# Attention block, one core: value products in two column halves of TensorE, in batches of one to five units, and VectorE normalising straight from PSUM

## The reference

```python
y = x * rsqrt(mean(x * x, -1) + eps) * rms_w           # x: 2 x 1024 x 512
y = einsum('bsm,cm->bsc', y, w_in)                      # 32 query heads, 8 groups of keys and values, 64 wide
q, k = rope(q), rope(k)
attn = softmax(where(causal, q @ k.T * 64 ** -0.5, -inf))
o = einsum('bghsp,bgxpd->bghsd', attn, v)               # the value products
x = layernorm(x + (x + einsum('bsc,mc->bsm', o, w_out)))
x = layernorm(x + einsum('bsd,od->bso', ternary(x), ternary(weight) + rram_variation))
```

## Time and profile before

| | us |
|---|---|
| median of 3 runs | 1411.08 (1410.71 to 1412.4) |
| the profiled execution | 1412.32 |
| its span, first to last instruction | 1410.5 |
| TensorE busy | 1290.8 (92%) |
| VectorE busy | 1182.6 (84%) |
| ScalarE busy | 1107.7 (79%) |
| GpSimd busy | 849.9 (60%) |

### The profile page before, as it was taken

The page is one execution under the profiler, slowest core; times in us unless marked ns, Lnnn a source line. Parts: engine busy times, 40 slices in busy tenths (PEclk is TensorE's granted clock), DMA queues, the critical chain, the costliest instruction groups (busy, mean ns, idle before and its releaser), DMA issues. The chain is left out here.

```text
span 1410.5 us, 25319 instructions
## 1 busy us (share of the span) xinstructions
PE 1290.8 (92%) x7328; PEld 757.5 (54%) x7328; DVE 1182.6 (84%) x3062; ACT 1107.7 (79%) x2327; POOL 849.9 (60%) x904
## 2 busy tenths in 40 slices
PE   4689998999989999999989999999989999898886
PEld 2355555555545555555645555555645555454554
DVE  4688887989898898988898898989898898888976
ACT  5768778788888888788888788788888888686654
POOL 1356666386746765376646766386646766785565
PEclk9799999999999999999999999999999999999999
DMA  6101111111101201111101211021101211110002
GB/s 201 27 20 44 59 31 32 29 55 46 39 20 47 59 27 31 29 56 46 38 21 46 59 29 31 24 61 45 37 22 42 59 33 50 50 44 25 19 32 86
DMA packets 45163, 61.82 MB, mean 44 GB/s; under 512 B 10464, under 2 KB 27104, under 8 KB 45024
## 3 DMA queue, kind: packets, MB, share of 16 engines
q1 hardware_dynamic: 45024, 60.20, 14.4%
HBM read 34.74 MB, written 4.46 MB: 28 GB/s over the span
## 5 line engine op out<-in xcount | busy, mean ns | idle before, releaser
L799 ACT ACTIVATE prob_hi<-t 128x512 f16<-128x512 f32 x576 | 340.2, 591 | 142.9 <-PE t L1225 137.8
L1104 DVE SCALAR_TENSOR_TENSOR prob_lo<-t,prob_hi 128x512 f16<-128x512 f32 x576 | 394.5, 686 | 58.8 <-ACT prob_hi L799 52.9
L831 ACT ACTIVATE prob<-prob,neg_max 128x896 f32<-128x896 f32 (+7 forms) x512 | 391.9, 767 | 8.9 <-DVE neg_max L1011 7.0
L1169 PE MATMUL s<-k_t,q_t 128*128 128x512 f16 (+3 forms) x1536 | 350.2, 330 | 32.3 <-DVE neg_max L1011 11.9
L1225 PE MATMUL t<-ident,prob 128*128 128x128 f32 x2304 | 351.5, 276 | 6.8 <-ACT prob L831 6.7
L1011 DVE CUSTOM_DVE_ANT_0 prob<-s,mask,neg_kappa 128x512 f32<-128x512 f32 (+3 forms) x512 | 320.0, 644 | 42.2 <-PE s L1169 24.8
L1225 PEld LDWEIGHTS t<-ident,prob 128*128 128x128 f32 x2304 | 290.5, 142 | 106.5 <-ACT prob L831 13.7
L1140 PE MATMUL ot<-prob_lo,v_sb 128*128 128x512 f16 x576 | 221.5, 385 | 29.8 <-DVE prob_lo L1104 28.9
L1138 PE MATMUL ot<-prob_hi,v_sb 128*128 128x512 f16 x576 | 220.4, 383 | 1.3 <-DVE o_raw L1085 1.0
L772 POOL TENSOR_TENSOR o_lo<-o_raw,o_hi 128x256 f16<-128x256 f32 x128 | 86.1, 672 | 196.3 <-ACT o_hi L907 194.7
L1169 PEld LDWEIGHTS s<-k_t,q_t 128*128 128x128 f16 x1536 | 137.5, 99 | 122.7 <-DVE neg_max L1011 37.2
(11 more groups left out here) (105 smaller groups left out, 1815.9 us busy)
## 6 DMA issues: line engine op xcount, KB each, us to landing
swapped<-flat SPq DMA_DIRECT2D x320, 64.0 KB, 2.0
spread<-recip_rows SPq DMA_DIRECT2D x128, 128.0 KB
recip_rows<-turned SPq DMA_DIRECT2D x512, 0.5 KB
raw<-L_attn_w_in SPq DMA_DIRECT2D x8, 768.0 KB, 4.2
raw<-L_attn_w_out SPq DMA_DIRECT2D x8, 512.0 KB, 3.6
out<-acc SPq DMA_DIRECT2D x16, 256.0 KB, 2.0
acc<-L_attn_x SPq DMA_DIRECT2D x3, 1024.0 KB, 10.4
acc<-L_attn_x SPq DMA_DIRECT2D x4, 256.0 KB, 3.2
```

The source lines that it names most:

```text
L799: act.activation(prob_hi[:, u % 2, :], t_ps[u % 2][:, :], ACT.Copy, scale=P_SCALE).then_inc(prob_hi_done, 1)
L831: act.activation(row, row, ACT.Exp, bias=neg_max[:, kk % 4, h:h + 1], scale=-1.0, accum_out=total[:, kk % 4, h:h + 1]).then_inc(ex_done, 1)
L1104: dve.scalar_tensor_tensor(out=prob_lo[:, u % 2, :], in0=t_ps[u % 2][:, :], scalar=P_SCALE, in1=prob_hi[:, u % 2, :], op0=ALU.mult, op1=AL ...
L1169: mm = pe.matmul(s_ps[:, off:off + cols], q_t[:, h, s * P:(s + 1) * P], k_t[:, part, keys:keys + cols], start=(part == 0), stop=(part == 1))
```

## The change

**The value product of a unit** is six matmuls in place of two. The stationary operand is 64 columns of `v_sb` (the high or the low part), the moving operand 256 of the 512 columns of `prob_hi` or `prob_lo`, and the result goes to partitions 0 to 63 (`a = 0`) or 64 to 127 (`a = 1`) of `ot_ps`, columns 0 to 255. The products are low part by `prob_hi`, high part by `prob_hi`, high part by `prob_lo`, each for both `a`; low part by `prob_lo` is no longer computed. All add into the same place, so the sum of high and low needs no later addition. The transposes put the heads in another order in `t_ps`, so that the columns fit.

**Batches.** `values` is called for several units at once, at the end of the slot behind the batch's last unit: `BATCHES` cuts the 36 units of a batch `b` into 1, 2, 3, 4, 5, 3+3, 4+3 and 4+4, so no batch of units crosses a tile. That makes 22 batches a body, 176 in all. `prob_hi` and `prob_lo` have eight buffers in place of two.

**Normalising.** `oe` and `o_low` are gone, and `on` moves from GpSimd to VectorE: one instruction of 128 partitions by 256 that reads `ot_ps`, scales it, multiplies by `spread` and writes `o_raw`. `oh` is as it was.

**Tables.** `OUTPUT` has three distances in place of four, and `rs` stands at most 20 steps behind `rc`.

```diff
+P_RING = 8
+BATCHES = (1, 2, 3, 4, 5, 3, 3, 4, 3, 4, 4)
...
+def batch_ending(u):
+
+    ends = list(itertools.accumulate(BATCHES))
+    return BATCHES[ends.index(u % UNITS + 1)] if u % UNITS + 1 in ends else 0
...
-    SCORES=(((0, 2, 2, 2), (3, 4, 6, 8), 24, 79), ((6, 7, 10, 24), (23, 29, 32, 36), 43, 114),
+    SCORES=(((0, 2, 2, 2), (3, 4, 6, 8), 24, 44), ((6, 7, 10, 24), (23, 29, 32, 36), 43, 63),
...
-        for kind, lag in zip(("oe", "on", "oh", "op"), at_pass["OUTPUT"][b * NT + s + 1]):
+        for kind, lag in zip(("on", "oh", "op"), at_pass["OUTPUT"][b * NT + s + 1]):
...
-                        elif e[0] == "on":
-                            _, b, s = e
-                            kk = b * NT + s
-
-                            wait(pool, o_raw_done, g, 2 * NT, kk + 1)
-                            wait(pool, spread_in[kk % 2], g, 16 * NT, 16 * (kk // 2 + 1))
-                            pool.tensor_tensor(o_raw[:, :, :], o_raw[:, :, :], spread[:, kk % 2, :, :], ALU.mult
-                                               ).then_inc(o_t_done, 1)
...
-                        wait(act, pv_done, g, BODY, u - 1)
-                        act.activation(prob_hi[:, u % 2, :], t_ps[u % 2][:, :], ACT.Copy, scale=P_SCALE
+                        wait(act, pv_done, g, BODY, u - P_RING + 1)
+                        act.activation(prob_hi[:, u % P_RING, :], t_ps[u % 2][:, :], ACT.Copy, scale=P_SCALE
                                        ).then_inc(prob_hi_done, 1)
...
-                        elif e[0] == "oe":
-                            _, b, s = e
-                            k = b * NT + s
-
-                            wait(act, pv_done, g, BODY, b * UNITS + first_unit(s + 1))
-                            wait(act, o_raw_done, g, 2 * NT, k)
-                            act.activation(o_low[:, :], ot_ps[k % 2][DH:P, :], ACT.Copy, scale=1.0 / P_SCALE
-                                           ).then_inc(o_low_done, 1)
...
-                        elif e[0] == "oe":
+                        elif e[0] == "on":
                             _, b, s = e
                             kk = b * NT + s
-                            wait(dve, o_low_done, g, 2 * NT, kk + 1)
+
+                            wait(dve, pv_done, g, BODY, b * UNITS + first_unit(s + 1))
+                            wait(dve, spread_in[kk % 2], g, 16 * NT, 16 * (kk // 2 + 1))
                             wait(dve, o_lo_done, g, 2 * NT, kk)
-                            top = ot_ps[kk % 2][0:DH, :].rearrange("p (c a q) -> p a c q", c=2, a=2)
-                            low = o_low[:, :].rearrange("p (c a q) -> p a c q", c=2, a=2)
-                            for a in range(2):
-                                mm = dve.scalar_tensor_tensor(out=o_raw[a * DH:(a + 1) * DH, :, :], in0=top[:, a],
-                                                              scalar=1.0 / P_SCALE, in1=low[:, a], op0=ALU.mult, op1=ALU.add)
-                            mm.then_inc(o_raw_done, 1)
+                            dve.scalar_tensor_tensor(out=o_raw[:, :, :],
+                                                     in0=ot_ps[kk % 2][:, 0:2 * P].rearrange("p (c q) -> p c q", c=2),
+                                                     scalar=1.0 / P_SCALE, in1=spread[:, kk % 2, :, :],
+                                                     op0=ALU.mult, op1=ALU.mult).then_inc(o_t_done, 1)
...
-                        wait(pe, o_raw_done, g, 2 * NT, k - 1)
-                    values_t = v_sb[:, b % 2, j, :]
-                    pe.matmul(ot_ps[k % 2][:, :], values_t, prob_hi[:, u % 2, :], start=(j == 0), stop=False)
+                        wait(pe, o_t_done, g, 2 * NT, k - 1)
+                    v_hi, v_lo = v_sb[:, b % 2, j, 0:DH], v_sb[:, b % 2, j, DH:P]
+
+                    def product(values_t, part, first, last):
+                        for a in range(2):
+                            mm = pe.matmul(ot_ps[k % 2][a * DH:(a + 1) * DH, 0:2 * P], values_t,
+                                           part[:, u % P_RING, a * 2 * P:(a + 1) * 2 * P], start=first, stop=last)
+                        return mm
+
+                    product(v_lo, prob_hi, j == 0, False)
+                    product(v_hi, prob_hi, False, False)
                     wait(pe, prob_lo_done, g, BODY, u + 1)
-                    pe.matmul(ot_ps[k % 2][:, :], values_t, prob_lo[:, u % 2, :], start=False, stop=(j == s)
-                              ).then_inc(pv_done, 1)
+                    product(v_hi, prob_lo, False, j == s).then_inc(pv_done, 1)
...
-                            mm = pe.transpose(t_ps[u % 2][:, h * P:(h + 1) * P],
+                            at = (h % 2 * 2 + h // 2) * P
+                            mm = pe.transpose(t_ps[u % 2][:, at:at + P],
                                               prob_row(s, h)[:, j * P:(j + 1) * P], ident[:, :])
...
                     if 0 < u <= plan.units or u == 0 and plan not in (first, opening):
-                        values(u - 1)
+                        for n in range(batch_ending(u - 1)):
+                            values(u - batch_ending(u - 1) + n)
```

More of the change, by code:

```diff
@@ L1 @@
+import itertools
 from contextlib import ExitStack
@@ L154 @@
     W_IN=(252, 263, 285, 295),
-    OUTPUT=((15, 12, 27, 45), (14, 26, 37, 70), (36, 54, 56, 69), (38, 38, 67, 92), (39, 41, 72, 93), (38, 47, 76, 114),
-         (31, 69, 86, 100), (34, 47, 54, 82), (17, 21, 27, 39), (22, 25, 34, 45), (24, 20, 34, 62), (23, 23, 43, 75),
-         (22, 23, 48, 65), (22, 26, 30, 52), (21, 41, 51, 84), (12, -1, 32, 61), (-128, 233, 117, 110)))
+    OUTPUT=((16, 27, 45), (26, 37, 70), (39, 56, 69), (38, 67, 92), (41, 72, 93), (47, 76, 114), (69, 86, 100), (47, 54, 82),
+     (21, 27, 39), (25, 34, 45), (20, 34, 62), (23, 43, 75), (23, 48, 65), (26, 30, 52), (41, 51, 84), (16, 32, 61),
+     (23, 117, 110)))
 FINAL = dict(
-    SCORES=(((0, 3, 11, 12), (9, 9, 11, 16), 29, 60), ((20, 22, 25, 32), (27, 28, 35, 38), 53, 67),
[10 rows of a table removed]
+    SCORES=(((0, 3, 11, 12), (9, 9, 11, 16), 29, 49), ((20, 22, 25, 32), (27, 28, 35, 38), 53, 67),
[10 rows of a table added]
     PROJECT=((((17, 27, 48, 142), (40, 28, 114, 193), (164, 169, 178, 201)), 150),
-         (((203, 209, 225, 258), (242, 248, 281, 315), (271, 265, 293, 317)), 261)),
+     (((203, 209, 225, 258), (242, 248, 281, 315), (271, 265, 293, 317)), 261)),
     NORM_O=(2, 14),
@@ L175 @@
     FFN_IN=((26, 63), (51, 119), (147, 190), (229, 270)),
-    OUTPUT=((13, 8, 20, 29), (15, 13, 26, 46), (23, 26, 26, 60), (30, 54, 60, 70), (30, 52, 52, 64), (21, 20, 60, 86),
-         (22, 21, 62, 72), (12, 35, 52, 84), (12, 18, 33, 53), (16, 27, 50, 69), (37, 42, 62, 76), (48, 52, 62, 92),
-         (52, 52, 75, 108), (36, 77, 85, 98), (49, 43, 55, 94), (34, 29, 35, 63), (18, 26, 34, 67)),
+    OUTPUT=((16, 20, 29), (16, 26, 46), (26, 26, 60), (47, 60, 70), (52, 52, 64), (20, 60, 86), (21, 62, 72), (35, 52, 84),
+     (18, 33, 53), (27, 50, 69), (39, 62, 76), (47, 62, 92), (52, 75, 108), (63, 85, 98), (43, 55, 94), (29, 35, 63),
+     (23, 34, 67)),
     LAYER=((317, 389, 407, 414, 419, 419, 449), (359, 392, 414, 431, 437, 444, 469), (388, 420, 437, 445, 450, 454, 474),
[5 rows of a table removed]
[5 rows of a table added]
 def body_plan(opening, last):
@@ L334, in seq_block @@
         prob = sb("prob", [P, P_SLOTS * BANK])
-        prob_hi = sb("prob_hi", [P, 2, BANK], F16)
-        prob_lo = sb("prob_lo", [P, 2, BANK], F16)
-        o_low = sb("o_low", [DH, BANK])
+        prob_hi = sb("prob_hi", [P, P_RING, BANK], F16)
+        prob_lo = sb("prob_lo", [P, P_RING, BANK], F16)
         o_raw = sb("o_raw", [P, 2, P])
@@ L414, in seq_block @@
         pv_done = sem("pv_done")
-        o_low_done = sem("o_low_done")
-        o_raw_done = sem("o_raw_done")
         o_t_done = sem("o_t_done")
@@ L648, in pool_idle @@
                     wait(pool, o_scale_done, g, 1, 1)
-                elif kind == "on":
-                    wait(pool, o_t_done, g, 2 * NT, what[0] * NT + what[1] + 1)
                 elif kind == "oh":
@@ L666, in one @@
                     for e in plan.ahead[u] + plan.behind[u]:
-                        if (e[0] not in ("ln", "res", "sq", "ro", "hl", "on", "oh", "fl", "x1", "nw", "no")
+                        if (e[0] not in ("ln", "res", "sq", "ro", "hl", "oh", "fl", "x1", "nw", "no")
                                 or plan is first and e[0] in ("ro", "hl")):
@@ L1102, in one @@
                         wait(dve, prob_hi_done, g, BODY, u + 1)
-                        wait(dve, pv_done, g, BODY, u - 1)
-                        dve.scalar_tensor_tensor(out=prob_lo[:, u % 2, :], in0=t_ps[u % 2][:, :], scalar=P_SCALE,
-                                                 in1=prob_hi[:, u % 2, :], op0=ALU.mult, op1=ALU.subtract
+                        wait(dve, pv_done, g, BODY, u - P_RING + 1)
+                        dve.scalar_tensor_tensor(out=prob_lo[:, u % P_RING, :], in0=t_ps[u % 2][:, :], scalar=P_SCALE,
```

(1 more changed line is left out.)

8 lines of the change are left out of this document (4 added, 4 removed), and 90 rows, old and new, of tables (LAYER, PROJECT, SCORES).

## The result

The changed kernel took 1448.11 us (median of four; the kernel before, on the same chip, 1411.74): ratio 1.0249, 95% interval 1.0226 to 1.0272. The prediction said 1396. The profiled execution took 1447.63, its span 1445.8.

The account below looks back on a forecast made before the run. The prediction took TensorE as the bound, 93% of a body being its own stream. Value products -58, passages +58 and less waiting -15 took 1412.3 to 1397, forecast as 1396 for the median; eight-in-ten range 1348 to 1475.

Parts of the forecast that it names:

- The value products: On TensorE: the two matmuls of a pair run beside each other, 0.33 us a unit in place of 0.43, -58 us.
- Rivals 3 and 4: Value products: 3, weight loads show, about 1480, chance 0.10; 4, halves don't run beside each other, 1557, chance 0.10.
- The passages: TensorE entering and leaving the halves, 352 times: each costs 0.165 us because it must first finish what is in flight, +58.
- rival 1: The passages between whole and halved array are nearly free: 1353, down to 1339 at no cost; chance 0.10.
- VectorE, ScalarE, GpSimd: New normalising instruction 415 ns; VectorE gives up 18 to 53 us, ScalarE 76.0, GpSimd 95.9; none enters the sum directly.
- New and old waits "about cancel": `o_raw`'s wait for GpSimd mostly goes; VectorE's for `spread` comes, losing 2.9 to 3.8 us once or twice a body.
- The wait for `prob_lo`: TensorE's wait for VectorE at the second value product: a third of 45 us counted as saved, -15.
- rival 2: Batches starve the engines in turn: TensorE stops between batches, VectorE runs dry in them; likeliest 1445, chance 0.24.

Follow-up runs that it names:

- e3: The changed kernel with full-width value products (two matmuls of 128 by 512) in its batches of up to five, addition of halves left out: 1460.48 us, ratio 1.0337.
- e2: The changed kernel with full-width value products, one unit at a time, addition of the halves left out: 1412.39 us, ratio 1.0002 to the kernel before.
- e5: e2 with VectorE's `on` reading a ready table in place of `spread`, so without waiting for that transfer; normalisation left out: 1387.62 us, ratio 0.9829.
- e7: Changed kernel, full-width products one unit at a time, `prob_lo` computed for 128 of 512 columns: 1383.36 us, ratio 0.9798.
- e8: e7 with the batches of up to five units put back: 1428.42 us, ratio 1.0116.
- e1: The kernel before with eight buffers of `prob_hi` and `prob_lo` and the changed kernel's batches, no halves: 1477.54 us, ratio 1.0458.
- e6: The changed kernel with full-width products and batches of at most two units, addition of the halves left out: 1406.87 us, ratio 0.9962.
- f2: The changed kernel with full-width products and batches of at most three units, addition of the halves left out: 1442.18 us, ratio 1.0216.
- f3: e3 with each batch cut in two, one half right behind the slot's transposes, the other at the slot's end: 1442.03 us, ratio 1.021.
- e4: The changed kernel with each batch moved behind the transposes of the next slot: 1445.63 us, ratio 1.0228.
- e10: e8 with `prob_hi` also cut to 128 columns and exponentials that don't sum: 1404.84 us, ratio 0.9952.
- f4: The changed kernel, complete, with e11's later `on` and batches of at most two units (320 batches): 1408.54 us, ratio 0.9976.
- f5: f4 with the odd tiles' single unit first, so that these tiles end with a pair: 1421.92 us, ratio 1.0068.
- e11: The changed kernel with `on` of tile (1, 2) 39 steps behind the tile's last unit in place of 23: 1434.98 us, ratio 1.0171.

## Why the prediction was wrong

**The value products: right.** Pairs run side by side, 0.33 us a unit, -58. Rivals 3 and 4 are refuted by the timeline, and nothing of two weight loads per 0.11 us shows. (The two matmuls of a pair do use the same 64 columns of `v_sb`, each with a load of its own; the prediction has it that they share no weights.)

**The passages: right, a little large.** 0.165 each was predicted, +58; 0.13 each is what the timeline has, +47. That rival 1 (nearly free) is wrong, the timeline and the 12.9 us show. The Trainium skill's rule, that a change of the tiling mode drains TensorE ("TensorEngine Tiling (Array Packing)", section "Key Properties"), agrees with the trace in that every passage has an extra step; the 0.13 is the runs' own, and less than the 0.165 at which the prediction priced the emptying.

**VectorE, ScalarE, GpSimd: right** in duration (418 ns) and in the signs.

**New and old waits "about cancel": wrong in size.** The prediction named the tile and the 2.9 to 3.8 us, and the trace has 2.75 at it. But the sum let the two waits cancel and gave the new one no price. Of the old wait 15.2 of the 39.1 us are still there, so it doesn't mostly go, and what the part that went had cost no run shows by itself. The new one stops VectorE with `prob_lo` and scores behind it. It cost 13 us in the changed kernel and 25 in full width.

**The wait for `prob_lo`, a third of 45 saved: this is the step that failed.** The sum had -15 for it, and gave the batches no price. The runs put +48 in its place (e3 against e2). The prediction had the sentence that a slot without a batch reaches the next transposes 0.43 us sooner, drew the mechanism out as rival 2 and priced it at 0.3 to 0.5 us a batch (48 / 144 = 0.33 is what was found), but gave it 0.24. Its forecast left those slots at nothing and kept VectorE's 5 to 6 us of relief a body as a gain. That relief is real where the wait for `spread` is gone (e5, 0.983 of the kernel before, some 24 us), but e7 and e8 show that relief of VectorE doesn't touch what the batches cost.

**The reckoning.** 1411.7 - 58 (halves) + 47 (passages) + 48 (batches) + 0 (what the relieved engines bring, some 24, less what the wait for `spread` takes, as much; e2 and e5) = 1449, against 1447.6 measured. The last two terms are differences of runs that end at e3, so they fit by construction; what is checked independently is the first two, -11 from the timeline against -12.9 from e3 to the changed kernel.

**The cause of the 48.** Shown: it comes with the batches alone, in either kernel (e1, e3); it is absent in e6 with at most two units and 30 of it is there in f2 with at most three; splitting a batch gives 18 back (f3), putting it behind the next transposes nothing clear of noise (e4); VectorE's pace has no part in it, shorter work on ScalarE takes about 20 off (e8, e10); and where in a tile the single unit stands is worth 13 us at equal sizes (f4, f5). Since f2 also ends its tiles with two or three units, some of its step from e6, perhaps those 13 of 35, can be that and not the size; no run separates them at full width. Argued only: with two banks for transposes and two for scores TensorE can be two units ahead, so that work put off for one unit comes back in time, and for two or more doesn't, whatever the pace of the others. The table of gaps fits this, as they lie ahead of transposes and scores, but no run has more banks. Open: why 26 us stay with short work on both engines (the gaps ahead of scores and transposes are where they lie), and why a tile that ends with a single unit is slower or faster; `oh`, `op` and the scores hang on the tile's last value product, and these runs don't separate them.

## What to carry to other kernels

Work that an engine can do while it waits for others is worth more than its own time. Bundling it to save a switching cost took it out of the places between the steps of a dependency chain, and cost 48 us, as much as the 47 of the switches that were left. Price the bundling by itself, with the work unchanged, and try the smallest bundle first: here two units were free at full width and up to three cost 30 us, and at equal sizes the place of the single unit made 13. When an operation moves to a busier engine, look up what it waited for on the old one: 2.75 us in one place of six bodies was 13 us in all, and a number in a table mended it.

## What the runs showed of the hardware

Two matmuls on the two column halves ran beside each other, 0.11 us for a pair of 256 columns, with two weight loads recorded at 0.11 each hidden behind them. Going from the whole array to halves cost 0.095 us at the step and 0.02 in the first unit, going back 0.10 at the step and 0.05 in the next four transposes. A transfer of 128 KB spread over the partitions let VectorE start 4.5 us after its issue (after, e2, and tile (1, 3) of e11), where the trace shows other DMAs of 64 KB landing in 2.0:

```profile
swapped<-flat SPq DMA_DIRECT2D x320, 64.0 KB, 2.0
```
